# Rebuilding the last network of a fused two-layer block from four barrier-separated blocks into three, with rounding moved to ScalarE

## What is computed

```python
def _act_fake_quant(x, clip_factor):
    scale = sigmoid(clip_factor) * max(abs(x)) / 127        # one maximum over all rows
    return clip(round(x / scale), -128, 127) * scale
def _weight_fake_quant(w):
    scale = max(abs(w), axis=1, keepdims=True) / 127        # one per row
    return clip(round(w / scale), -128, 127) * scale
xq   = _act_fake_quant(layernorm(x), clip_x[0])
gate = xq @ _weight_fake_quant(w_gate).T                    # 4096 x 704
up   = xq @ _weight_fake_quant(w_up).T
h    = _act_fake_quant(silu(gate) * up, clip_down[0])
x    = x + tanh(g_ffn[1]) * (h @ _weight_fake_quant(w_down).T)
```

## Time and profile before

| | us |
|---|---|
| median of 3 runs | 2190.08 |
| profiled execution, its own time | 2192.67 |
| its span on the core | 2191.0 |
| all before the last network (up to the first operation of its layernorm) | 1978.6 |
| layernorm, weights, maximum of x, up to the first scale | 57.2 |
| rounding and transposing x (f2, second part) | 21.5 |
| gate, up, silu, product, maximum (f3) | 69.4 |
| second scale | 3.4 |
| rounding h, last product, sum (f4) | 57.4 |
| end of the last store | 3.5 |

### The profile page before, as it was taken

How to read it: one execution, slowest core, us unless ns; L and a number is a source line. 1 busy time by engine, 2 the same in 40 slices (tenths; PEclk the granted TensorE clock), 3 DMA queues, 4 the chain that set the end, 5 groups by cost and what they waited for, 6 DMA issues and landing times. The chain is left out here.

```text
span 2191.0 us, 45917 instructions
## 1 busy us (share of the span) xinstructions
PE 1753.9 (80%) x14366; PEld 1166.3 (53%) x14375; DVE 1444.2 (66%) x2967; ACT 1075.1 (49%) x2519; POOL 1037.8 (47%) x1535
## 2 busy tenths in 40 slices
PE   0588888884279889999968999999989999991467
PEld 0344444442235556666646776667667777771223
DVE  4356676775974434444436877877877788876686
ACT  1256666664622212222214666666666666671563
POOL 1555565641817723223236565656665666540005
PEclk9689999997579989999989999999999999995686
DMA  3000000002800012222114322322222223301002
GB/s 104 12 7 13 13 10 10 10 1 79 246 13 1 1 63 65 67 70 71 58 51 104 78 71 69 82 71 67 67 70 68 68 72 80 78 20 40 0 0 77
DMA packets 89215, 117.59 MB, mean 54 GB/s; under 512 B 16392, under 2 KB 58640, under 8 KB 89104
## 3 DMA queue, kind: packets, MB, share of 16 engines
q1 hardware_dynamic: 76048, 90.08, 15.5%
q0 software_dynamic: 6528, 17.83, 3.0%
q10 hardware_dynamic: 6528, 8.39, 1.1%
HBM read 56.36 MB, written 17.83 MB: 34 GB/s over the span
## 5 line engine op out<-in xcount | busy, mean ns | idle before, releaser
L1069 POOL TENSOR_SCALAR a_P<-a_P,a_RS 128x256 f32<-128x256 f32 x512 | 254.8, 498 | 235.9 <-DVE a_RS L1351 206.5
L1238 ACT ACTIVATE a_P<-a_pS,a_NM 128x256 f32<-128x256 f32 x512 | 237.8, 471 | 199.7 <-DVE a_NM L1347 196.0
L815 DVE TENSOR_REDUCE a_M<-a_pS 128x2 f32<-128x512 f32 x256 | 164.8, 686 | 140.1 <-PE a_pS L626 138.9
L1247 ACT ACTIVATE a_PH<-a_pT 128x512 f16<-128x512 f32 x256 | 154.1, 602 | 78.9 <-PE a_pT L1163 68.7
L1347 DVE TENSOR_REDUCE a_NM<-a_pS 128x2 f32<-128x512 f32 x256 | 175.0, 684 | 26.5 <-PE a_pS L1155 21.0
L1357 DVE TENSOR_TENSOR a_PL<-a_pT,a_PH 128x512 f16<-128x512 f32 x256 | 172.8, 675 | 15.4 <-ACT a_PH L1247 15.3
L754 ACT ACTIVATE a_PT<-a_pT 128x512 f32<-128x512 f32 x256 | 139.1, 599 | 73.2 <-PE a_pT L645 73.2
L1163 PE MATMUL a_pT<-g_ident,a_P 128*128 128x128 f32 x1024 | 155.3, 275 | 20.9 <-POOL a_P L1069 20.9
L1163 PEld LDWEIGHTS a_pT<-g_ident,a_P 128*128 128x128 f32 x1024 | 119.8, 141 | 38.7 <-POOL a_P L1069 19.2
L1946 ACT ACTIVATE me_hh<-me_pH 128x512 f16<-128x512 f32 x72 | 43.0, 597 | 175.6 <-PE me_pH L1933 156.1
L99 PE MATMUL a_pF<-a_ch,xw_XW 128*128 128x256 f16 x512 | 102.8, 285 | 32.3 <-DVE a_VL L1339 29.2
(11 more groups left out here) (427 smaller groups left out, 5256.1 us busy)
## 6 DMA issues: line engine op xcount, KB each, us to landing
a_KD<-a_KN SPq DMA_DIRECT2D x128, 128.0 KB
a_QS<-a_QN SPq DMA_DIRECT2D x128, 128.0 KB
mr_stage<-mw SPq DMA_DIRECT2D x24, 512.0 KB, 4.8
ys<-me_yb SPq DMA_DIRECT2D x72, 128.0 KB
a_ctxin<-ctxT SPq DMA_DIRECT2D x32, 256.0 KB, 2.8
a_KZ<-a_KN SPq DMA_DIRECT2D x64, 128.0 KB
g_X<-x SPq DMA_DIRECT2D x1, 4096.0 KB, 15.1
rows<-mr_row ACTq DMA_DIRECT2D x32, 128.0 KB, 3.7
```

Source lines behind the costliest of these rows:

```text
L815: nc.vector.reduce_max(M[:, :, a, p2], pS[a][:], AX.X).then_inc(s_max.sem, 1)
L1069: last = nc.gpsimd.tensor_scalar(P32[u % 4][:, a, :], P32[u % 4][:, a, :], RS[u % 4][:, a:a + 1], LIFT, ALU.mult, ALU.mult)
L1238: last = nc.scalar.activation(P32[u % 4][:, a, :], pS[u % 2][:, a, :], ACT.Exp, bias=NM[u % 4][:, a:a + 1], accum_out=SM[u % 4][:, a:a + 1])
L1247: nc.scalar.activation(PH[p2 % 2][:, :, :, j * P:(j + 1) * P].rearrange("p a k q -> p (a k) q"), pT[u % 2][:].rearrange("p a k q -> p (a k ...
```

## The change

Everything before the last network is untouched. `layernorm_stats`, `quant_weights` and the four stages become three stages.

**Opening.** The layernorm, the loads, the weights and the maximum of x are one stage. The loads are issued at its start, and VectorE waits for each weight by itself. ScalarE normalises x (32 activations) instead of VectorE; the overall maximum is taken in two halves, the first between the second and the third weight. The weights' working tiles lie in HT's memory.

**Inner.** The rounding and transposing of x is inside the loop over blocks, one block ahead: while block n is multiplied, block n + 1 is rounded. Both the lift and the lowering are on ScalarE, and one VectorE pass clamps from both sides.

**Last.** The blocks are cut into halves of 256 rows throughout: ScalarE lifts and lowers each half, VectorE clamps once, TensorE waits only for the same half of the block before, and each half has its own store.

```diff
-            dve.wait_ge(loaded, 80)
+                        dve.wait_ge(loaded[n], 16 if n == 2 else 32)
...
+                    def normalise(half):
+                        for t in range(half * TILES // 2, (half + 1) * TILES // 2):
+                            ins = nc.scalar.activation(XN[:, t, :], X[:, t, :], ACT.Identity, bias=nb[:, t:t + 1], scale=rstd[:, t:t + 1])
+                        ins.then_inc(xn_done, 1)
...
+                    dve.wait_ge(padded, 6)
+                    quantise(0, nat[0], q[0], sg[:])
+                    quantise(1, nat[1], q[1], su[:])
+                    largest(0)
+                    quantise(2, natd, qd, mx[2][:, 0:KD])
...
+                    largest(1)
...
+                    transposes(0)
+                    with pe.Fori(0, NBLK - 1) as n:
+                        for m in range(IT):
+                            if m == 4:
+                                transposes(n + 1)
+                            step(n, m)
...
+                    def unround(n):
+                        rounded.wait(act, n, 1)
+                        xt_full.wait(act, n, 0)
+                        act.nop(nofuse=True)
+                        xv = XN[:, bass.ts(n, TB), :].rearrange("p t d -> p (t d)")
+                        nc.scalar.activation(qv, xv, ACT.Identity, bias=unrounder[:]).then_inc(unrounded.sem, 1)
...
+                    def clamp(n):
+                        unrounded.wait(dve, n, 1)
+                        V.tensor_scalar(qv, qv, QMAX, -QMAX - 1.0, ALU.min, ALU.max).then_inc(q_ready.sem, 1)
...
+                        for m in range(IT):
+                            silu(n, m)
+                            if m == 0:
+                                round_block(n + 1)
+                            elif m == 1:
+                                unround(n + 1)
+                            elif m == 4:
+                                keep(n + 1)
...
+                        for m in range(IT):
+                            product(n, m)
+                            if m:
+                                largest(n, m - 1)
+                            if more and m == 2:
+                                clamp(n + 1)
...
+                def lifted(n, half):
+                    nc.scalar.activation(part(n, half), part(n, half), ACT.Identity, bias=rounder[:], scale=inv[:, 1:2]).then_inc(h_rounded.sem, 1)
+
+                def lowered(n, half):
+                    h_rounded.wait(act, n, half + 1)
+                    y_full.wait(act, n, half - 1)
+                    act.nop(nofuse=True)
+                    nc.scalar.activation(HQ[half][:], part(n, half), ACT.Identity, bias=unrounder[:]).then_inc(capped.sem, 1)
+
+                act.wait_ge(h_scaled, 1)
+                lifted(0, 0)
+                with act.Fori(0, NBLK - 1) as n:
+                    lifted(n, 1)
+                    lowered(n, 0)
+                    lifted(n + 1, 0)
+                    lowered(n, 1)
```

More of the change, by code:

```diff
@@ L2150, in scale_steps @@
-    def scale_steps(name, which, col):
-        row, top = s.sb(f"{name}row", [1, P]), s.sb(f"{name}top", [1, 1])
-        pR, pB = s.ps(f"{name}pR", [1, P]), s.ps(f"{name}pB", [P, 1])
-        col_ready, row_full, top_ready, all_full, st = (s.sem(f"{name}{x}") for x in ("col", "rowf", "topr", "allf", "st"))
+    sg, su, sgx, sux = (s.sb(n, [P, IT]) for n in ("sg", "su", "sgx", "sux"))
+    clip, sig, scale, inv = (s.sb(n, [P, 2]) for n in ("clip", "sig", "scale", "inv"))
+    lift = s.sb("lift", [1, P])
@@ L2156, in on_pe, with scale_steps @@
+    y_full, scaled, added = s.counter("y_full", 2, 2), s.counter("scaled", 2, 2), s.counter("added", 2, 2)
+    stored = s.sem("stored")
+    def scale_steps(ctx, name, which, col):
+        part = Scope(nc, ctx, f"f{name}")
+        top = part.sb("top", [1, 1])
+        pR, pB = part.ps("pR", [1, P]), part.ps("pB", [P, 1])
+        col_ready, row_full, top_ready, all_full, steps = (part.sem(x) for x in ("col", "rowf", "topr", "allf", "steps"))
         def on_pe(pe):
@@ L2159, in on_pe, with on_dve @@
             pe.wait_ge(top_ready, 1)
-            nc.tensor.matmul(pB[:], ones[:], top[:], start=True, stop=True).then_inc(all_full, 1)
-        def on_dve(dve, scale_done):
-            ch = Chain(st, 0)
+            nc.tensor.matmul(pB[:], lift[:], top[:], start=True, stop=True).then_inc(all_full, 1)
+        def on_dve(dve, done):
+            ch = Chain(steps, 0)
             ch.begin(0)
@@ L2376, in _, with clamp, results @@
-                with dve.Fori(0, NBLK // 2 - 1) as i:
-                    for q in range(2):
-                        round_block(i * 2 + 2 + q, q)
-                        results(i * 2 + 1 + q)
-                results(NBLK - 1)
+                def clamp(n, half):
+                    capped.wait(dve, n, half + 1)
+                    hq = HQ[half][:].rearrange("p m t -> p (m t)")
+                    V.tensor_scalar(hq, hq, QMAX, -QMAX - 1.0, ALU.min, ALU.max).then_inc(hq_ready.sem, 1)
+                def results(n, half):
+                    y_full.wait(dve, n, half + 1)
+                    added.wait(dve, n, half - 1)
+                    V.tensor_tensor(y[half][:], pY[half][:], row_scale[:].unsqueeze(1).broadcast_to([P, 2, D]), ALU.mult).then_inc(scaled.sem, 1)
@@ L2382, in _ @@
+                clamp(0, 0)
+                clamp(0, 1)
+                dve.wait_ge(row_ready, 1)
+                with dve.Fori(0, NBLK - 1) as n:
+                    for half in range(2):
+                        results(n, half)
+                        clamp(n + 1, half)
+                for half in range(2):
+                    results(NBLK - 1, half)
             @block.gpsimd
```

515 lines of the change are left out of this document (238 added, 277 removed).

## The result

The change took the median from 2193.76 us (four runs, 2186.51 to 2199.95) to **2164.22 us** (four runs, 2159.77 to 2166.69): ratio 0.9866, interval 0.984 to 0.9892.

What follows compares the result with a forecast made beforehand. VectorE was taken to bound the opening and inner blocks, TensorE at 1.2 GHz the last phase. Terms -19.8 + 2.3 + 2.5 - 1.3 = -16.3 us, from the median of 2190.08, gave 2174 us, range 2165 to 2183.

Steps and rivals of the forecast that it cites:

- the fall of the clock: Inner part: TensorE's clock falls behind its wait for the clamp in four blocks of ten, +2.5 us.
- TensorE as a second pace-maker of the last phase: Last phase: ScalarE and TensorE at 1.2 GHz both pace it, at about 6.3 us a block.
- Opening: -19.8 forecast: Up to the first scale: 57.2 becomes 37.4 us, with less load wait, fewer stage changes and no VectorE normalising.
- The step of S: Opening: VectorE's first operation S starts 1.2 us later, as sixteen counter starting values are added before it.
- Inner part: +4.8 forecast with the clock: First scale to maximum of h: 90.9 becomes 93.2 us, +2.3, and +2.5 for the clock.
- the walk: Inner part: one block followed through the engines' crossed waits, sixth product at 10.4 us, taken as 10.7 a block.
- Table loads: nothing: Inner part: removing seven table loads gains nothing, since VectorE idled only 1.8 us beside them.
- Last part: -1.3 forecast: Last phase -0.5 us, change of stage -0.4, last store -0.4; ends -4 and +4.
- Rival 1: Inner part: the low clock holds throughout, +9.6 instead of +2.5, 2181 us, chance 0.12.
- rival 2: Inner part: the gap brings the low clock in each block, 2178 us, chance 0.12.
- Rival 3: Inner part: waits do not cross as walked, VectorE stays the bound at 8.3 us a block, 2155 us, chance 0.06.
- Rival 4: Inner part: TensorE at 1.2 GHz still waits 2.3 us for the clamp, 13.6 us a block, 2194 us, chance 0.04.

Runs made afterwards that it cites:

- e3: Changed kernel with VectorE instead of ScalarE lowering the second half of each block in the last phase: 2158.18 us.
- e4: Changed kernel with the later inner rounding of e2 and the shared last-phase lowering of e3 together: 2160.50 us.
- e11: Changed kernel with the edits of e1 and e3 together: 2150.84 us.
- e14: Changed kernel with the edits of e12 and e3 together: 2147.48 us, ratio to before 0.9794.
- e5: Changed kernel with four filler VectorE passes ahead of the clamp of each inner block but the first: 2178.37 us.
- e8: Changed kernel with the inner part's lowering back on VectorE, in two passes with the clamp, and ScalarE's left out: 2176.55 us.
- e7: Changed kernel with ScalarE's inner list as a loop over blocks instead of seven unrolled copies, so table loads return: 2166.61 us.
- e2: Changed kernel with inner lift, lowering behind silus 2, 3, clamp behind product 3, transposes at the block's end, copy behind silu 5: 2160.24 us.
- e12: Changed kernel with lift, lowering and transposes of the next block each one tile later in the inner part: 2153.30 us.
- e1: Changed kernel with the next block's transposes ahead of inner tile 5 instead of 4: 2151.89 us.
- e15: Changed kernel with inner lift and lowering after tiles 2 and 3, clamp after the fourth product, transposes ahead of the sixth tile: 2154.04 us.

## Why the prediction was wrong

The waits that set the pace were the ones walked, and nearly every size was too dear, all in one direction: -16.3 us were forecast and the stages give -30.1. Wrong in kind were the fall of the clock, which did not come, and TensorE as a second pace-maker of the last phase. That the time is 9.8 us from the forecast and not 13.8 is luck: the kernel before had a median of 2190.08 when I forecast and 2193.76 beside after.

- **Opening: -19.8 forecast, -22.0 measured.** The step of S was right in size, 1.17 where I took 1.2 (2.44 for 1.27). The kernels with two counters more (e3, e4, e11, e14) start 0.11 later again, 2.55; at that price sixteen counters are 0.9 of the 1.17, an estimate. First weight 0.6 earlier. The two 6.41 us for a weight were wrong to carry over: six scalings took 2.29 us before, each linked to the next by a semaphore, and 1.67 after, where only the last is linked, twice, 0.6 each. The kernel's code showed that, and I had not priced it. ScalarE was ahead as walked, its operations 0.50 us apart where I took 0.59.
- **Inner part: +4.8 forecast with the clock, -2.9 measured.** This is the step that failed, by 7.7 us: the price of a block in the walk, and the clock term. "First gate product and table load 2.2" was 1.3, because the load ran beside the product; "first block at the low clock up to its sixth product 10.7" was 9.4, because the clock rose early in it and not at its end; "six blocks of 10.7" were 6 x 10.25. The walk itself gave 10.4; the 0.3 that I added for its error on the old block were not due. The last block (7.67 for 7.8) and the end were right.
- **The clock: +2.5 forecast, nothing measured.** It fell in none of the seven blocks, whose gaps were 1.93 and 1.27 us where I had walked one of 2.3. That was a choice between ends of 0 and +9.6 which the two gaps of the earlier trace rows could not narrow. (The +9.6 itself does not come out of its terms: 1.1 us in six or seven blocks and 2.6 in the last are 9.2 or 10.3.) e5 and e8 show the term real, with falls behind gaps of 3.27 and 2.30 us, and e7 shows three behind 1.93. What spared after is not shown.
- **Table loads: nothing, and the rows bear that out** for the kernel before, though no run shows it alone. e7 shows that they would not have stayed free.
- **Last part: -1.3 forecast, -5.1 measured.** ScalarE 48.5 us and not 50.9: the lift was right (1654 ns for 1.66 us), the lowering follows after 1.46 us, and the register steps that I added cost nothing beside it. TensorE does not set the pace with it, as I had it: its clock was at a mean of 0.81, and it was busy for 34.7 of the 54.2 us. Second scale -1.1 where I took -0.4, store and end -0.8 for -0.4.

**The rivals.** Rival 1 (low clock throughout) and 2 (low clock in each block) did not come; e2, e5 and e8 are what rival 2 describes, one reordering or one pass away. The Trainium skill, "TensorE: Matmul & The Clock Gate", section "HAM oscillation", describes a loop whose own wait brings the low clock back each round: e2 and e5 agree, with 0.52 for 3.4 us in each block of e2, and so does e4 from its second block on, while after, with 1.93 us of waiting in each, holds 1.00. Rival 3, with VectorE as the bound at 8.3 us a block, is what e12 comes near by another order: 8.67 us, with VectorE busy for 8.12 of them. Rival 4 did not come, though with 12.7 us a block e5 nearly gave it.

**The range.** Its low end was the sum of the cheap ends that I had stated: -22, +2.3, 0 and -4 make 2166, and I stated 2165. What it lacked is an end for the inner walk, the one term that I bounded by nothing below +2.3 but a rival at 8.3 us a block. The walk as it stood, 10.4 without the correction, and the load beside the gate product would have taken 3 us off, and the stated low end to 2162. And the dear choices were not independent: load wait, weights, walk, register steps and clock all leaned the same way.

## What to carry to other kernels

Where engines wait for each other across a loop, walk one round with durations from rows before and after a change: the walk was within 0.5 us of the block in six orders, and it shows which single wait to move (one number, e1: 6.9 us). Then look at TensorE's granted clock in each candidate by itself, since the order that walks best may be the one in which it falls in every round, as in e2. And a term that comes from a walk needs a low end like any other: leave out each correction and each step that may run beside another, and see where the sum goes.

## What the runs showed of the hardware

- Six like VectorE operations in a row took 1.67 us without a semaphore between them (after) and 2.29 with one in each (before).
- ScalarE's time for 1536 elements lay on the line that I drew through 1024 and 3072, 0.83 ns an element: 1.65 us with scale and bias, and 1.56 with bias alone. Operations of 256 elements came 0.50 us apart, where the line has 0.59 for one.
- VectorE's clamp of 1536 elements took 0.56 us alone and 1.50 beside GpSimd's addition, which took 1.80 there instead of 1.27 (e3, seven of eight blocks). In after fifteen clamps took 0.56 and the last, beside an addition, 1.56.
- The granted clock stayed at 1.00 through seven blocks with gaps of 1.93 and 1.27 us (after), and did either behind 1.93 us in e7, behind 1.63 in e15 and behind 1.30 in e4.
